# A block attention stage rebuilt around quarter-height matmuls, in an eight-layer kernel on one core

## The chip, the cores and the metric

The kernel runs on one core of one Trainium2 chip. The metric is the device time of one execution in microseconds (us), here the median of three. A core has five engines with queues of their own: TensorE (PE), VectorE (DVE), ScalarE (ACT), GpSimd (POOL) and SyncE (SP), which here only starts transfers.

## The reference

The program is a stack of eight layers over x, 16 batches of 128 tokens by 128 features, with a second input of the same shape as context. The layer that matters here is the second block attention (`L1_xattn`), third in the kernel's count (`layer2`). Its input is the normalised x for the queries and the context for keys and values. There are 16 heads of width 8. For each head and each of the two blocks of 64 keys a softmax of its own is taken, and the two results are added with the weights 1 and 2:

```
q = norm(x) @ Wq * 8**-0.5 ; k = ctx @ Wk ; v = ctx @ Wv         (16 heads of 8)
for each batch, head, block g of 64 keys:
    s = q @ k[g].T ;  p = exp(s - max(s)) ;  o_g = (p @ v[g]) / sum(p)
x += gate * ((o_0 + 2 * o_1) @ Wo)
```

The layer before it (`layer1`) is a small feed-forward layer (128 to 512 to 128), the one after it (`layer3`) a feed-forward layer with eight compared branches.

## The kernel before

Everything is written by hand: each engine has one list of instructions, and semaphores join them. Features lie on the 128 partitions and tokens in the free dimension, so xT is 128 by 2048, cut into four chunks of 512 (one PSUM bank of f32). PSUM has eight banks, `bank(0)` to `bank(7)`.

Each layer begins with `pe_norm`, `act_norm` and `dve_norm`: two matmuls per chunk (L192, L197), three ACT passes (L207, L211, L212) and one DVE product (L218).

`layer2` then projects keys and values (L538, L540) and splits k into a high and a low f16 part (L632 on ACT, L669 on DVE). To give each of the 16 heads its own rows, `spread_keys` writes, per batch and part, a 128 by 2048 f16 table of k times a head mask, on POOL (L623; on DVE for batch 0). POOL also carries one row gather (an indirect DMA, L808) ahead of each table: these 128 gathers in all fill `pe`, which `layer3` turns (L834) and `layer4` uses. POOL waits for the landing of one before it starts the next.

The attention runs in 32 half steps (`t`), each with 8 heads of one batch. A half step is: scores on PE (L571, 6 matmuls of 512 columns, tokens of the queries on partitions), maximum and subtraction on DVE (L682, L685), exp on ACT (L663), 8 transposes on PE (L581), two copies on ACT (L652), 8 matmuls of 18 columns on PE (L601) into `pv`. Per batch DVE then divides and adds (L695 to L699). Every four batches a query projection (L562), four transposes (L588) and the output projection (L593) come in between. `TURNS` is the order in which banks 4 and 5 are filled and copied.

Of the kernel before, what the change touches and what calls it, by code (L numbers as in the profile page):

```python
# [5 lines left out]
B, S, D = 16, 128, 128  # L6
# [27 lines left out]
def flamingo_kernel(nc, ins, out, stop=LAYERS):  # L34
# [5 lines left out]
    with ExitStack() as ctx:  # L40
# [16 lines left out]
        consts = sb("consts", [128, 5 * 128 + NH1 + 2 * NH2 + CAP + NH2 // 2])  # L57
# [3 lines left out]
        l1x_w = sb("l1x_w", [D, 4 * D])  # L61
# [37 lines left out]
        hm4 = consts[:, 640 + NH1 + 2 * NH2 + CAP:640 + NH1 + 2 * NH2 + CAP + NH2 // 2]  # L99
        l0f_w1 = work[:, 11264:11264 + F]  # L100
# [56 lines left out]
        A2 = sems("attn2", "vset k_ps v_ps k low v kblk s exp_in exp fill filled pv o")  # L157
# [16 lines left out]
        CEN = (4, 0, 0, 0, 4, 0, 3, 0)  # L174
        VAR = (2, 4, 6, 6, 0, 6, 0, 4)
# [266 lines left out]
        def pe_layer1(te):  # L442
            pe_norm(te, 1)
            loaded(te, "l0f")
            for c in range(NCH + 1):
                if c < NCH:
                    for f in range(FT):
                        if c:
                            te.wait_ge(F1["act"], FT * (c - 1) + f + 1)
                        te.matmul(bank(f), l0f_w1[:, f * 128:(f + 1) * 128], nT[:, cs(c)],  # L450
                                  start=True, stop=True).then_inc(F1["up"], 1)
                if c:
# [10 lines left out]
        def act_layer1(act, link):  # L463
# [7 lines left out]
            for c in range(NCH + 1):  # L471
                if c < NCH:
                    for f in range(FT):
                        act.wait_ge(F1["up"], FT * c + f + 1)
                        if c >= 2:
                            act.wait_ge(F1["down"], c - 1)
                        act.activation(hq[:, c % 2, f, :], bank(f), ACT.Relu, bias=col("l0f_b1", f),
                                       saturate=False).then_inc(F1["act"], 1)
                if c:
# [6 lines left out]
        def dve_layer1(dve, link):  # L486
            dve_norm(dve, 1)
            for c in range(NCH + 1):
                if c:
# [10 lines left out]
        WEIGHT1 = 2.0  # L500
        VW = 2 * (HD1 + 1)
        vext = wA[:, 0:B * NH1 * VW].rearrange("p (b h w) -> p b h w", b=B, h=NH1)
        kT = wA[:, B * NH1 * VW:B * NH1 * VW + T].bitcast(f16).rearrange("p (r n) -> p r n", r=2)
        qT = nT[:].bitcast(f16).rearrange("p (c r n) -> p c r n", c=NCH, r=2)
        kblk = work[:, 0:4096].bitcast(f16).rearrange("p (s r h k) -> p s r h k", s=2, r=2, h=NH1)
        Q_SCALE = HD1 ** -0.5
        pr = work[:, 4096:8192].rearrange("p (r h k) -> p r h k", r=2, h=NH1)
        prT = work[:, 8192:12288].rearrange("p (r h q) -> p r h q", r=2, h=NH1)
        mx = sm(0, NH1 * NBLK // 2)
        rs = sm(32, NH1 * NBLK)  # L510
        o_a = sm(64, 128).rearrange("p (h w) -> p h w", h=NH1)
        o_b = sm(192, 128).rearrange("p (h w) -> p h w", h=NH1)
        otok = sm(512, 512).rearrange("p (b d) -> p b d", b=BC)
        oT = sm(1024, 512)
        y2 = sm(1536, 512)

        HH = NH1 // 2
        STEPS = 2 * B
        CS = 2 * BC
        TURNS = []  # L520
        for _t in range(STEPS + 5):
            if _t == 0 or _t < STEPS - 1 and _t % CS == CS - 1:
                TURNS.append((_t, ("q", (_t + 1) // CS)))
            if 2 <= _t < STEPS + 2:
                TURNS += [(_t, ("t", _t - 2, j)) for j in range(2)]
            if _t >= CS + 3 and (_t - 3) % CS == 0:
                TURNS.append((_t, ("o", (_t - 3) // CS - 1)))
            if _t >= CS + 4 and (_t - 4) % CS == 0:
                TURNS.append((_t, ("y", (_t - 4) // CS - 1)))

        def fill_at(*what):
            return [w for _, w in TURNS].index(what) + 1

        def pe_layer2(te):
            pe_norm(te, 2)
            loaded(te, "l1x")
            for c in range(NCH):
                te.matmul(bank(c), l1x_w[:, D:2 * D], cT[:, cs(c)], start=True, stop=True).then_inc(A2["k_ps"], 1)  # L538
            for b in range(B):
                mm = te.matmul(bank(4 + b // BC)[:, (b % BC) * D:(b % BC + 1) * D], cT[:, tok(b)],  # L540
                               l1x_w[:, 2 * D:3 * D], start=True, stop=True)
                if b % BC == BC - 1:
                    mm.then_inc(A2["v_ps"], 1)
            te.wait_ge(A2["low"], NCH)
            te.wait_ge(A2["v"], 2 * NCH)

            def fill(*what):
                n = fill_at(*what) - 1
                if n >= 2:
                    te.wait_ge(A2["filled"], n - 1)  # L550
                    last = TURNS[n - 2][1]
                    if last[0] == "q":
                        te.wait_ge(A2["low"], NCH + last[1] + 1)
                return bank(4 + n % 2)


            for t in range(STEPS + 5):
                if t < STEPS:
                    b, j = t // 2, t % 2
                    if (t, ("q", (t + 1) // CS)) in TURNS:  # L560
                        c = (t + 1) // CS
                        te.matmul(fill("q", c), l1x_w[:, 0:D], nT[:, cs(c)], start=True, stop=True).then_inc(A2["fill"], 1)  # L562
                    if t % CS == 0:
                        te.wait_ge(A2["low"], NCH + t // CS + 1)
                    if b:
                        te.wait_ge(A2["kblk"], b)
                    if t >= 2:
                        te.wait_ge(A2["exp_in"], t - 1)
                    for n in range(2):
                        for i, (p, r) in enumerate(PARTS):  # L570
                            mm = te.matmul(bank(2 * j + n), qT[:, b // BC, p, b % BC * S:(b % BC + 1) * S],  # L571
                                           kblk[:, b % 2, r, HH * j + 4 * n:HH * j + 4 * n + 4, :], start=(i == 0), stop=(i == 2))
                    mm.then_inc(A2["s"], 1)
                if 2 <= t < STEPS + 2:
                    u = t - 2
                    a, j = u // 2, u % 2
                    te.wait_ge(A2["exp"], u + 1)
                    for n in range(2):
                        dst = fill("t", u, n)
                        for h in range(4):  # L580
                            mm = te.transpose(dst[:, h * S:(h + 1) * S], pr[:, a % 2, HH * j + 4 * n + h, :], ident)  # L581
                        mm.then_inc(A2["fill"], 1)
                if t >= CS + 3 and (t - 3) % CS == 0:
                    c = (t - 3) // CS - 1
                    te.wait_ge(A2["o"], BC * (c + 1))
                    dst = fill("o", c)
                    for n in range(BC):
                        mm = te.transpose(dst[:, n * S:(n + 1) * S], otok[:, n, :], ident)  # L588
                    mm.then_inc(A2["fill"], 1)
                if t >= CS + 4 and (t - 4) % CS == 0:  # L590
                    c = (t - 4) // CS - 1
                    te.wait_ge(A2["filled"], fill_at("o", c))
                    te.matmul(fill("y", c), l1x_w[:, 3 * D:4 * D], oT, start=True, stop=True).then_inc(A2["fill"], 1)  # L593
                if 3 <= t < STEPS + 3:
                    u = t - 3
                    a, j = u // 2, u % 2
                    te.wait_ge(A2["filled"], fill_at("t", u, 1))
                    if a >= 2 and j == 0:
                        te.wait_ge(A2["o"], a - 1)
                    for h in range(HH * j, HH * (j + 1)):  # L600
                        mm = te.matmul(bank(6 + a % 2)[:, h * VW:(h + 1) * VW], prT[:, a % 2, h, :], vext[:, a, h, :],  # L601
                                       start=True, stop=True)
                    if j:
                        mm.then_inc(A2["pv"], 1)

        def pool_layer2(pool, link):
            pool.wait_ge(s_x, NCH)
            link(pool.memset(wA[:, 0:B * NH1 * VW], 0.0))
            link(pool.memset(vext[0:64, :, :, HD1:HD1 + 1], 1.0))
            pool.memset(vext[64:128, :, :, VW - 1:VW], 1.0).then_inc(A2["vset"], 1)  # L610
            for b in range(1, B):
                pool.wait_ge(A2["low"], b // BC + 1)
                if b >= 2:
                    pool.wait_ge(A2["s"], 2 * (b - 1))
                spread_keys(pool, b).then_inc(A2["kblk"], 1)
            pool_gather(pool, IN_L0 + 2 * (B - 1), S)

        def spread_keys(eng, b):
            for r in range(2):
                if b:  # L620
# [1079 lines left out]
```

## Time and profile before

| | |
|---|---|
| time, median of 3 | 1003.61 us (1000.99 to 1004.13) |
| the profiled execution: its time, its span | 1002.72 us, 1000.7 us |
| PE, DVE, ACT, POOL busy | 87%, 66%, 58%, 35% of the span |
| mean granted TensorE clock | 0.921 of full speed |
| `layer1` from its first matmul | 235.7 us |
| `layer2`: norm begins, norm ends | 255.0 us, 264.6 us |
| first score, begin of the next layer | 277.1 us, 450.6 us |

The span is from the first to the last instruction; the execution's own time is 2.0 us longer. Starts are in microseconds from the start of the span. A f32 matmul stands in the trace as two records, a f16 matmul as one. PEld is the load of a matmul's fixed operand, which overlaps PE. The granted clock is 1.00 at 2.4 GHz and 0.50 at 1.2 GHz.

### The profile page before, as it was taken

The page shows a single profiled execution, that of the slowest core. Times are in us where ns is not written, and L with a number is a line of the kernel's source. Part 1 is how long each engine was busy: PE and PEld are TensorE (multiplying, and loading weights), DVE is VectorE, ACT ScalarE, POOL GpSimd, SP SyncE. Part 2 cuts the span into 40 slices and gives each one's busy share as a digit, 9 for nine tenths or more (in the row PEclk, how much of TensorE's full clock was granted, in tenths as well). Part 3 has the DMA queues.
Part 4 walks back from the last instruction along what each step waited for, and adds up shares of the span by engine and source line. Part 5 has one row for each costly group of instructions (what it writes and reads, how often), then busy time and mean ns, then how long its engine had stood idle before and what let it go on. Part 6 is the DMA issues. An engine that isn't in the chain of part 4 may idle for free.

```text
span 1000.7 us, 13965 instructions
## 1 busy us (share of the span) xinstructions
PE 872.9 (87%) x5417; PEld 574.6 (57%) x5417; DVE 663.9 (66%) x979; ACT 580.6 (58%) x994; POOL 354.2 (35%) x254
## 2 busy tenths in 40 slices
PE   4899999999779888999997699996889887989776
PEld 1576777763347667674555675553568764444322
DVE  3886767651557677654887667885677426776667
ACT  4797878756734444435447233453568565576464
POOL 1123233331589799833333022105693003000003
PEclk9899999998979799889998799887799998999888
DMA  6210000006000000000000000005000000000001
GB/s 215 63 61 20 20 22 23 23 22 95 9 14 14 11 14 14 14 22 24 21 25 1 1 1 1 1 1 213 0 1 1 2 1 0 1 0 1 1 0 42
DMA packets 12848, 25.35 MB, mean 25 GB/s; under 512 B 3560, under 2 KB 4848, under 8 KB 12528
## 3 DMA queue, kind: packets, MB, share of 16 engines
q1 hardware_dynamic: 8688, 16.07, 5.6%
q0 software_dynamic: 4096, 8.40, 3.3%
q8 instruction: 43, 0.70, 0.3%
q14 instruction: 21, 0.17, 0.1%
HBM read 23.41 MB, written 1.05 MB: 24 GB/s over the span
## 4 chain that ended last, share of the span: by engine, by line
PE 61%; DVE 22%; ACT 11%; issue 3%; POOL 1%; DMA 1%; SPq 0%; POOLq 0%; DVEq 0%; ACTq 0%
PE ps L317 8%; PE ps L289 8%; PE ps L728 6%; PE ps L601 4%; PE ps L571 4%; PE ps L867 3%; PE ps L192 2%; PE ps L581 2%; PE ps L1219 2%; DVE big L954 2%; PE ps L1189 2%; ACT nT L211 2%; ACT nT L212 2%; PE ps L450 2%; PE ps L197 1%
## 5 line engine op out<-in xcount | busy, mean ns | idle before, releaser
L808 POOL DMA_INDIRECT pe<-in_rpe,idx x128 | 132.6, 1036 | 274.2 <-DMA pe<-in_rpe,idx 197.2
L359 DVE TENSOR_TENSOR big<-l1f_w,big 128x512 f16<-128x512 f32 x128 | 87.3, 691 | 42.2 <-ACT big L346 39.7
L623 POOL TENSOR_TENSOR big<-big,consts 128x2048 f16<-128x2048 f16 x30 | 109.8, 3659 | 0.6
L345 ACT ACTIVATE l1f_w<-ps,wcols 128x512 f32<-128x512 f32 x128 | 90.1, 704 | 29.7 <-PE ps L289 27.2
L317 PEld LDWEIGHTS ps<-big 128*128 128x128 f16 x1536 | 89.8, 99 | 12.4 <-DVE big L359 5.3
L317 PE MATMUL ps<-big 128*128 128x128 f16 x1536 | 92.6, 221 | 4.7 <-DVE big L359 4.7
L289 PE MATMUL ps<-vx,big 128*128 128x512 f16 x384 | 91.6, 390 | 2.7 <-DVE nT L218 2.7
L346 ACT ACTIVATE big<-ps,wcols 128x512 f16<-128x512 f32 x128 | 90.6, 708 | 0.0
L601 PEld LDWEIGHTS ps<-big 128*128 128x128 f32 x512 | 66.1, 208 | 1.8 <-issue 1.0
L601 PE MATMUL ps<-big 128*128 128x18 f32 x512 | 65.1, 272 | 0.0
L289 PEld LDWEIGHTS ps<-vx,big 128*128 128x128 f16 x384 | 37.5, 101 | 44.0 <-issue 4.6
L652 ACT ACTIVATE big<-ps 128x512 f32<-128x512 f32 x64 | 35.5, 594 | 46.5 <-PE ps L581 46.5
L682 DVE TENSOR_REDUCE small<-ps 128x16 f32<-128x1024 f32 x32 | 39.0, 1220 | 31.4 <-PE ps L571 31.1
L728 PE MATMUL ps<-nT,l1f_w 128*128 128x512 f32 x128 | 57.7, 593 | 2.2 <-DVE nT L218 2.2
L1484 POOL TENSOR_TENSOR big<-l1f_w,big 128x512 f16<-128x512 f32 x8 | 10.6, 1331 | 138.4 <-ACT big L1521 138.4
L571 PE MATMUL ps<-big,nT 128*128 128x512 f16 x192 | 54.8, 430 | 5.0 <-POOL big L623 2.2
L663 ACT ACTIVATE big<-big 128x1024 f32<-128x1024 f32 x32 | 33.8, 1056 | 36.4 <-DVE big L685 36.4
L192 PE MATMUL ps<-xT,consts 128*128 128x512 f32 x64 | 40.2, 735 | 11.4 <-DMA xT<-in_xT 9.9
L936 ACT ACTIVATE big<-ps,small 128x128 f32<-128x128 f32 x128 | 34.9, 380 | 25.7 <-PE ps L894 25.7
L218 DVE TENSOR_TENSOR nT<-ps,nT 128x512 f32<-128x512 f32 x32 | 22.1, 691 | 40.8 <-ACT nT L212 40.7
L825 POOL TENSOR_TENSOR big<-nT,consts 128x512 f32<-128x512 f32 x16 | 16.8, 1059 | 83.2 <-PE ps L884 43.8
L581 PE MATMUL ps<-consts,big 128*128 128x128 f32 x256 | 38.5, 298 | 5.4 <-DVE nT L676 5.3
(307 smaller groups left out, 1869.4 us busy)
## 6 DMA issues: line engine op xcount, KB each, us to landing
big<-in_l0x_w SPq DMA_DIRECT2D x16, 256.0 KB, 3.3
pe<-in_l2f_w SPq DMA_DIRECT2D x16, 256.0 KB, 6.5
pe<-in_rpe,idx POOLq DMA_INDIRECT x128, 2.6
cT<-in_cT SPq DMA_DIRECT2D x1, 1024.0 KB, 9.7
l1f_w<-in_l1f_w SPq DMA_DIRECT2D x1, 1024.0 KB, 5.1
vx<-in_ctok SPq DMA_DIRECT2D x1, 1024.0 KB, 16.5
out_xT<-xT SPq DMA_DIRECT2D x4, 256.0 KB, 2.2
xT<-in_xT SPq DMA_DIRECT2D x1, 768.0 KB, 7.1
```

The costliest lines, as they stand in the source:

```text
L192: te.matmul(bank(CEN[i] + c), centre_w, xT[:, cs(c)], start=True, stop=True).then_inc(s_cen, 1)
L289: mm = te.matmul(bank(f), w16[:, e, a, f * 128:(f + 1) * 128], x16[:, c, b, :], start=(n == 0), stop=(n == 2))
L317: mm = te.matmul(bank(4 + k % 2)[:, t * D:(t + 1) * D], h16[:, k % 2, a, f, t * S:(t + 1) * S], w16[:, k % E, b, F + f * D:F + (f + 1) * D ...
L345: act.activation(h32[:, f, :], bank(f), ACT.Relu, bias=b, scale=1 / W_UP)
L346: act.activation(h16[:, k % 2, 0, f, :], bank(f), ACT.Relu, bias=b, scale=1 / W_UP).then_inc(M0["act"], 1)
L359: dve.tensor_tensor(h16[:, k % 2, 1, f, :], h32[:, f, :], h16[:, k % 2, 0, f, :], SUB).then_inc(M0["lo"], 1)
L571: mm = te.matmul(bank(2 * j + n), qT[:, b // BC, p, b % BC * S:(b % BC + 1) * S], kblk[:, b % 2, r, HH * j + 4 * n:HH * j + 4 * n + 4, :], ...
L581: mm = te.transpose(dst[:, h * S:(h + 1) * S], pr[:, a % 2, HH * j + 4 * n + h, :], ident)
L601: mm = te.matmul(bank(6 + a % 2)[:, h * VW:(h + 1) * VW], prT[:, a % 2, h, :], vext[:, a, h, :], start=True, stop=True)
L623: ins_ = eng.tensor_tensor(kblk[:, b % 2, r, :, :], kT[:, r, tok(b)].unsqueeze(1).to_broadcast([128, NH1, S]), hm16.unsqueeze(2).to_broadc ...
L728: mm = te.matmul(bank(at + r), l1f_w[:, w * D:(w + 1) * D], nT[:, cs(2 * (k // NC) + r)], start=True, stop=True)
L808: pool.indirect_dma_start(out=pe[:, v * D:(v + 1) * D], out_offset=None, in_=ins["rpe"], in_offset=bass.IndirectOffsetOnAxis(ap=idx[:, v:v ...
```

## The change

1. **Keys and values** are projected in `layer1`, after each chunk's four first matmuls (`pe_keys`, `dve_keys`). v is written once per key block, zero outside of it (16 columns a head instead of 18, without columns of ones).
2. **Scores in row groups.** The 16 heads are cut into four quarters `t` of four heads, which lie on 32 partitions each (`quad(t)`). k and q are spread with a mask over four heads (tables of 128 by 1024, both parts in one instruction, both on POOL). A score matmul has K = 32 rows, 512 columns, and bank `t`.
3. **Second scores.** The first scores are only used for the maxima (`dve_reduce`). PE turns the 8 maxima of each quarter into rows (`pe_maxima`), DVE spreads them with a minus sign (`dve_maxima`, mblk), and the scores are computed again with keys on partitions (`pe_turned`), with a fourth, f32 matmul that adds minus the maximum. ACT takes exp straight from PSUM (banks 4 and 5). Subtraction, transposes and copies are gone.
4. **Values in column groups.** 16 matmuls (M = 16, 128 columns, f32) and 4 for the sums (M = 32, 512 columns, f32) write the partitions 32t to 32t + 31 of banks 6 and 7. DVE takes the reciprocal of all 128 by 512 sums and multiplies.
5. **Projection.** The output stands transposed already; it is projected by 4 f32 matmuls of 512 columns per four batches, against weights with each row of Wo laid out twice, and added to x from PSUM.
6. Banks of the norm of `layer3` are changed; three constant tables and the three further weight blocks are loaded with the others (170 and 384 columns more).

```diff
-        CEN = (4, 0, 0, 0, 4, 0, 3, 0)
-        VAR = (2, 4, 6, 6, 0, 6, 0, 4)
+        CEN = (4, 0, 0, 4, 4, 0, 3, 0)
+        VAR = (2, 4, 6, 2, 0, 6, 0, 4)
...
+        def pe_keys(te, c):
...
+            te.matmul(bank(6), l1x_w[:, D:2 * D], cT[:, cs(c)], start=True, stop=True).then_inc(A2["proj_ps"], 1)
+            for t in range(BC):
+                mm = te.matmul(bank(7)[:, t * D:(t + 1) * D], cT[:, tok(c * BC + t)], l1x_w[:, 2 * D:3 * D], start=True, stop=True)
+            mm.then_inc(A2["proj_ps"], 1)
...
+        def pe_scores(te, b, t, part):
+            p, r = PARTS[part]
+            return te.matmul(bank(t), qT[quad(t), b // BC, p, b % BC * S:(b % BC + 1) * S], kblk[quad(t), b % KS, r, :, :],
+                             start=(part == 0), stop=(part == 2))
+
+        def pe_turned(te, b, t, part):
+            if part == 3:
+                return te.matmul(bank(4 + t % 2), to_keys[quad(t), :], mblk[quad(t), b % 2, :, :], start=False, stop=True)
+            p, r = PARTS[part]
+            return te.matmul(bank(4 + t % 2), kT[quad(t), p, tok(b)], qblk1[quad(t), b % QS, r, :, :],
+                             start=(part == 0), stop=False)
+
+        def pe_maxima(te, b):
+            te.wait_ge(A2["mx"], 2 * b + 2)
+            te.transpose(bank(2)[:, 0:128], mxp[:, b % 2, :, :].rearrange("p t w -> p (t w)"), ident).then_inc(A2["mT"], 1)
+
+        def pe_values(te, b):
+            te.wait_ge(A2["exp"], 2 * b + 2)
+            if b:
+                te.wait_ge(A2["on"], b)
+            for j in range(4):
+                for t in range(4):
+                    te.matmul(bank(6)[32 * t:32 * t + 2 * HD1, j * S:(j + 1) * S], vext[:, b, 4 * t + j, :], pr[:, b % 2, t, j, :],
+                              start=True, stop=True)
+            for t in range(4):
+                mm = te.matmul(bank(7)[quad(t), :], sum_w, pr[:, b % 2, t, :, :], start=True, stop=True)
+            mm.then_inc(A2["pv"], 1)
...
+            for b in range(B + 2):
+                if b + 2 < B and (b + 2) % BC == 0:
+                    te.wait_ge(A2["mx"], 2 * b + 3)
+                    pe_queries(te, (b + 2) // BC)
+                if b >= BC + 1 and (b - BC - 1) % BC == 0:
+                    if b + 1 < B:
+                        te.wait_ge(A2["mx"], 2 * b + 3)
+                    pe_project(te, (b - BC - 1) // BC)
+                if b < B:
+                    te.wait_ge(A2["mblk"], b + 1)
+                    te.wait_ge(A2["qblk"], b + 1)
+                    if b:
+                        te.wait_ge(A2["exp"], 2 * b)
+                    for part in range(4):
+                        for t in (0, 1):
+                            mm = pe_turned(te, b, t, part)
+                        if part == 3:
+                            mm.then_inc(A2["st"], 1)
+                        elif b + 1 < B:
+                            for t in (2, 3):
+                                mm = pe_scores(te, b + 1, t, part)
+                            if part == 2:
+                                mm.then_inc(A2["s"], 1)
+                if 1 <= b <= B:
+                    pe_values(te, b - 1)
+                if b + 1 < B:
+                    pe_maxima(te, b + 1)
+                if b < B:
+                    te.wait_ge(A2["exp"], 2 * b + 1)
...
+                    for part in range(4):
+                        for t in (2, 3):
+                            mm = pe_turned(te, b, t, part)
...
+                            for t in (0, 1):
+                                mm = pe_scores(te, b + 2, t, part)
...
+                for u in range(2):
+                    act.wait_ge(A2["st"], 2 * b + u + 1)
+                    act.activation(pr[:, b % 2, 2 * u:2 * u + 2, :, :].rearrange("p t j q -> p (t j q)"), ps[:, 2048:3072],
+                                   ACT.Exp).then_inc(A2["exp"], 1)
...
+            for b in range(B + 2):
+                if b + 2 < B and (b + 2) % BC == 0:
+                    dve_queries(dve, (b + 2) // BC)
+                if b >= BC + 1 and (b - BC - 1) % BC == 0:
+                    c = (b - BC - 1) // BC
+                    dve.wait_ge(A2["y_ps"], c + 1)
+                    dve.scalar_tensor_tensor(xT[:, cs(c)], bank(0), gt[:, 2:3], xT[:, cs(c)], MUL, ADD).then_inc(s_x, 1)
+                if b + 1 < B:
+                    dve_reduce(dve, b + 1, 1)
+                    dve_maxima(dve, b + 1)
+                if 1 <= b <= B:
+                    a = b - 1
                     dve.wait_ge(A2["pv"], a + 1)
...
+                    link(dve.reciprocal(rsum, bank(7)))
+                    dve.tensor_tensor(on[:, a // BC % 2, :, a % BC, :], bank(6).rearrange("p (j q) -> p j q", j=4),
+                                      rsum.rearrange("p (j q) -> p j q", j=4), MUL).then_inc(A2["on"], 1)
+                if b + 2 < B:
+                    dve_reduce(dve, b + 2, 0)
```

PE's order at the heart of `layer2` before, two and a half half steps (L571 the scores, L581 the transposes of the exponentials, L601 the values):

```order
L571 MATMUL ps<-big,nT 128x512 x6
L581 MATMUL ps<-consts,big 128x128 x8
L601 MATMUL ps<-big 128x18 x8
L571 MATMUL ps<-big,nT 128x512 x6
L581 MATMUL ps<-consts,big 128x128 x8
```

And PE's order in the same place now, from the end of the first bundle of batch 1 to the queries ahead of batch 2 (L557 the f32 matmul of the maxima, L572 and L575 values and sums of batch 0, L564 the transpose of the maxima of batch 2, L559 the turned scores of batch 1, L552 the first scores of batch 3, L548 a query projection):

```order
L557 MATMUL ps<-big,consts 128x512 x2
L572 MATMUL ps<-big 16x128 x16
L575 MATMUL ps<-big,consts 32x512 x4
L564 MATMUL ps<-consts,small 128x128
L559 MATMUL ps<-big 128x512 x2
L552 MATMUL ps<-big,nT 128x512 x2
L559 MATMUL ps<-big 128x512 x2
L552 MATMUL ps<-big,nT 128x512 x2
L559 MATMUL ps<-big 128x512 x2
L552 MATMUL ps<-big,nT 128x512 x2
L557 MATMUL ps<-big,consts 128x512 x2
L548 MATMUL ps<-nT,l1x_w 128x512
```

Before, the three kinds of work of a half step follow each other. Now turned scores and first scores alternate two by two in a bundle that ends with the two f32 matmuls of the maxima, values and sums stand between the two bundles of a batch, and a projection stands ahead of the first.

DVE's order now in the same place (L703 half of the maxima, L709 mblk, L735 and L736 the division, L699 the low part of a chunk of queries):

```order
L703 TENSOR_REDUCE small<-ps 128x2x8
L699 SCALAR_TENSOR_TENSOR nT<-ps,nT 128x512
L703 TENSOR_REDUCE small<-ps 128x2x8
L709 TENSOR_TENSOR big<-ps,consts 128x512
L735 RECIPROCAL small<-ps 128x512
L736 TENSOR_TENSOR big<-ps,small 128x4x128
L703 TENSOR_REDUCE small<-ps 128x2x8 x2
```

The division, a reciprocal of 32 columns before, is now one of 512, and it stands ahead of the reduction of the next scores.

## Rows read from the trace of the kernel before

**Rows 1.** The page, busy time of each engine and what shares the chain that ended last.

```profile
PE 872.9 (87%) x5417; PEld 574.6 (57%) x5417; DVE 663.9 (66%) x979; ACT 580.6 (58%) x994; POOL 354.2 (35%) x254
...
PE 61%; DVE 22%; ACT 11%; issue 3%; POOL 1%; DMA 1%; SPq 0%; POOLq 0%; DVEq 0%; ACTq 0%
```

**Rows 2.** The chain that ended last, `layer2` to the next layer: start, length, what.

```profile
264.58 3.71 PE ps L538 x8
...
269.64 6.80 DVE big L623 x2
...
277.10 4.23 PE ps L571 x12
...
305.46 1.30 PE ps L571 x6
...
450.63 3.41 PE ps L192 x4
```

**Rows 3.** Timeline of PE in `layer2`: start, length, instruction, idle before it.

```profile
317.18 1.86 PE L601 MATMUL ps<-big 128*128 128x18 f32 x16
...
321.05 1.86 PE L601 MATMUL ps<-big 128*128 128x18 f32 x16
...
331.53 1.12 PE L588 MATMUL ps<-consts,small 128*128 128x128 f32 x4 [2.57 <-DVE small L699]
332.44 3.44 PE L601 MATMUL ps<-big 128*128 128x18 f32 x16
```

**Rows 4.** Windows of 2 us: length, PE busy (instructions), granted clock, DMA share, GB/s.

```profile
332.00:334.00 2.00, 2.00 (x12) 0.50 0.13 33
...
338.00:340.00 2.00, 2.00 (x10) 0.50 0.09 23
...
354.00:356.00 2.00, 0.00 (x0) 1.00 0.00 0
...
360.00:362.00 2.00, 2.00 (x9) 0.51 0.04 10
```

**Rows 5.** Timeline of POOL at the end of `layer2` and in `layer3`.

```profile
417.20 0.99 POOL L808 DMA_INDIRECT pe<-in_rpe,idx  x1 [0.16 <-issue]
418.21 3.61 POOL L623 TENSOR_TENSOR big<-big,consts 128x2048 f16<-128x2048 f16 x1
...
426.76 0.98 POOL L808 DMA_INDIRECT pe<-in_rpe,idx  x1 [0.16 <-issue]
...
522.65 0.94 POOL L808 DMA_INDIRECT pe<-in_rpe,idx  x1 [1.90 <-DMA pe<-in_rpe,idx]
```

**Rows 6.** Groups by line on PE: shapes, records | busy us, mean ns | idle.

```profile
L317 PE MATMUL ps<-big 128*128 128x128 f16 x1536 | 92.6, 221 | 4.7 <-DVE big L359 4.7
...
L540 PE MATMUL ps<-l1x_w,cT 128*128 128x128 f32 x32 | 3.7, 275 | 0.0
L538 PE MATMUL ps<-cT,l1x_w 128*128 128x512 f32 x8 | 3.7, 605 | 2.2 <-DVE nT L218 2.2
```

**Rows 7.** Window of `layer1`: PE, PEld, DVE, ACT, POOL busy, clock, DMA share, GB/s.

```profile
235.70:255.00 19.30, 19.26 (x49) 8.52 (x50) 1.76 (x3) 13.16 (x20) 4.87 (x6) 0.91 0.31 35
```

**Rows 8.** Groups by line on DVE.

```profile
L682 DVE TENSOR_REDUCE small<-ps 128x16 f32<-128x1024 f32 x32 | 39.0, 1220 | 31.4 <-PE ps L571 31.1
...
L695 DVE RECIPROCAL small<-ps 128x32 f32<-128x32 f32 x16 | 5.7, 358 | 16.6 <-PE ps L601 16.1
...
L669 DVE TENSOR_TENSOR big<-ps,big 128x512 f16<-128x512 f32 x4 | 2.8, 692 | 2.3 <-ACT big L632 2.2
...
L1445 DVE RECIPROCAL small<-small 128x4 f32<-128x4 f32 x12 | 2.1, 178 | 0.4
```

**Rows 9.** The exponential, ACT in `layer2`.

```profile
L663 ACT ACTIVATE big<-big 128x1024 f32<-128x1024 f32 x32 | 33.8, 1056 | 36.4 <-DVE big L685 36.4
```

**Rows 10.** The chain that ended last, the last matmuls of `layer3` before the sixteenth turn (L834).

```profile
526.86 3.45 PE ps L728 x8
```

More of the change, by code:

```diff
@@ L156, in flamingo_kernel @@
         F1 = sems("ffn1", "w2q up act down o16")
-        A2 = sems("attn2", "vset k_ps v_ps k low v kblk s exp_in exp fill filled pv o")
+        A2 = sems("attn2", "proj_ps hi low v kblk qblk s mx mT mblk st exp pv on y_ps")
         F3 = sems("ffn3", "sel comp take best cand picked")
@@ L512, in flamingo_kernel @@
[L512 to L529, printed above, removed]
@@ L531, in fill_at @@
-        def fill_at(*what):
-            return [w for _, w in TURNS].index(what) + 1
+        KS, QS = 3, 2
+        qblk1 = work[:, 0:1024].bitcast(f16).rearrange("p (s r j q) -> p s r j q", s=QS, r=2, j=4)
+        mblk = work[:, 1024:2048].rearrange("p (s j q) -> p s j q", s=2, j=4)
+        kblk = work[:, 2560:4096].bitcast(f16).rearrange("p (s r j k) -> p s r j k", s=KS, r=2, j=4)
+        pr = work[:, 4096:8192].rearrange("p (s t j q) -> p s t j q", s=2, t=4, j=4)
+        on = work[:, 8192:12288].rearrange("p (s j b q) -> p s j b q", s=2, j=4, b=BC)
@@ new lines, in pe_queries @@
+        def pe_queries(te, c):
+            te.matmul(bank(1), l1x_w[:, 0:D], nT[:, cs(c)], start=True, stop=True).then_inc(A2["proj_ps"], 1)
+        def pe_scores(te, b, t, part):
[8 more added lines that the diff above has]
+                             start=(part == 0), stop=False)
@@ L534, in pe_layer2, with pe_project @@
+        def pe_project(te, c):
+            te.wait_ge(A2["on"], BC * (c + 1))
+            for j in range(4):
+                mm = te.matmul(bank(0), l1x_w[:, (3 + j) * D:(4 + j) * D], on[:, c % 2, j, :, :], start=(j == 0), stop=(j == 3))
+            mm.then_inc(A2["y_ps"], 1)
         def pe_layer2(te):
+            te.wait_ge(A2["low"], NCH)
+            te.wait_ge(A2["v"], NCH)
             pe_norm(te, 2)
-            loaded(te, "l1x")
-            for c in range(NCH):
-                te.matmul(bank(c), l1x_w[:, D:2 * D], cT[:, cs(c)], start=True, stop=True).then_inc(A2["k_ps"], 1)
@@ L539, in pe_layer2 @@
-            for b in range(B):
[L540 to L554, printed above, removed]
@@ L557, in pe_layer2 @@
[L557 to L604, printed above, removed]
@@ L618, in spread_keys @@
[L618 to L625 removed]
+            pe_queries(te, 0)
+            te.wait_ge(A2["low"], NCH + 1)
@@ new lines, in pe_layer2 @@
+            te.wait_ge(A2["v"], NCH)
+            te.wait_ge(A2["kblk"], 1)
+            for u in range(2):
+                for part in range(3):
+                    for t in (2 * u, 2 * u + 1):
+                        mm = pe_scores(te, 0, t, part)
+                mm.then_inc(A2["s"], 1)
+            te.wait_ge(A2["kblk"], 2)
+            te.wait_ge(A2["mx"], 1)
+            for part in range(3):
+                for t in (0, 1):
+                    mm = pe_scores(te, 1, t, part)
+            mm.then_inc(A2["s"], 1)
@@ new lines, in pool_layer2 @@
+        def pool_layer2(pool, link):
+            for b in range(KS - 1):
+                pool_keys(pool, b)
+            for b in range(B):
+                if b:
+                    v = IN_L0 + 2 * (b - 1)
+                    pool_gather(pool, v, v + 1)
+                if b + KS - 1 < B:
+                    pool_keys(pool, b + KS - 1)
+                if b:
+                    pool_gather(pool, v + 1, v + 2)
+                pool.wait_ge(A2["low"], NCH + b // BC + 1)
+                if b >= QS:
+                    pool.wait_ge(A2["st"], 2 * (b - QS) + 2)
+                pool_spread(pool, qblk1[:, b % QS, :, :, :],
+                            qT[:, b // BC, :, b % BC * S:(b % BC + 1) * S]).then_inc(A2["qblk"], 1)
+            pool_gather(pool, IN_L0 + 2 * (B - 1), S)
@@ L665, in dve_layer2, with dve_maxima @@
+        def dve_maxima(dve, b):
+            dve.wait_ge(A2["mT"], b + 1)
+            dve.tensor_tensor(mblk[:, b % 2, :, :], bank(2)[:, 0:128].unsqueeze(1).to_broadcast([128, 4, S]),
+                              minus4.unsqueeze(2).to_broadcast([128, 4, S]), MUL).then_inc(A2["mblk"], 1)
         def dve_layer2(dve, link):
             dve_norm(dve, 2)
-            for c in range(NCH):
-                dve.wait_ge(A2["k"], c + 1)
-                dve.tensor_tensor(kT[:, 1, cs(c)], bank(c), kT[:, 0, cs(c)], SUB).then_inc(A2["low"], 1)
```

191 lines of the change are left out of this document (94 added, 97 removed).

## The prediction

> **What bounds the kernel now.** I read first the page's chain: PE holds 61% of it and is busy for 87% of the span [rows 1], so the reader is to look at what PE does, and at what it waits for where it does not. The chain in order of time gives the piece that the change rebuilds: the norm of `layer2` ends at 264.58, the next layer begins at 450.63, which is 186.1 us [rows 2]. Within it the first score starts at 277.10: 3.71 us of key projections, then 6.80 us in which DVE spreads the keys of batch 0 [rows 2]. From there 173.5 us go to 16 batches, 10.8 us for each.
>
> Three things share these 10.8 us. PE alone needs less: undisturbed half steps start 3.87 us apart (317.18 and 321.05), 7.75 us a batch [rows 3]. POOL needs 9.56 us: from the gather at 417.20 to the one at 426.76 lie two gathers of 0.99 and two tables of 3.61 us with hardly a pause [rows 5]. And PE pays for pauses twice. It waited 2.57 us at 331.53, and 16 records of L601 then took 3.44 us where they take 1.86 [rows 3]; the clock stayed at half from 332 to 340 [rows 4]. It idled from 354 to 356 and ran at half at 360 [rows 4]. So the stage is held by POOL and by restarts, with PE close behind.
>
> **Part 1, the start.** Keys and values move into `layer1`: 8 records of L538 in 3.7 us, 32 of L540 in 3.7 us [rows 6]. PE is busy there for 19.26 of 19.30 us [rows 7], so all 7.4 us are paid. ACT's four copies and DVE's eight new passes are covered: ACT has 6 us free and DVE 17 [rows 7]. In exchange `layer2` starts sooner. From the end of the norm: a query projection 0.86 (two records of 0.43, from L538's 3.44 for 8 in steady flow, here 3.7 with the first one's start, [rows 6]), a copy and the low part 0.6 + 0.7, two bundles of first scores with three reductions of 1.22 behind them, mblk 0.69 [rows 8], and about 0.9 us of handing over: the loop begins 7.8 us behind the norm. POOL's first tables are made before that, beside the norm.
>
> **Part 2, what a batch costs on PE.** I count slots. A f16 matmul of 512 columns takes 0.216 (six in 1.30, [rows 2]), a f32 one of 512 columns 0.86 and one of 128 columns 0.233 (both L538 and L540, [rows 6]); the last two stand in the trace as two records each, one behind the other. One after another the new batch would need 24 x 0.216 for scores, 4 x 0.86 for the maxima, 16 x 0.233 for values, 4 x 0.86 for sums, 0.1 for the transpose: 15.9 us. That is twice today's 7.75. The whole change rests on matmuls in different quarters of the array running at once, and no row here shows that. The bounds: each waits for the one before (0.216 us apart), or only issue counts, of which L317 gives 0.060 us (1536 records in 92.6 us, [rows 6]). I take the low end for f16, since nothing that two such matmuls share (queue, weight load) takes longer than those 0.060: a round of four costs one slot, 0.22 to 0.24.
>
> For f32 I take less, and this is the choice that decides. PE starts its matmuls in the order of the program. The second record of quarter 0 has to wait for the first one on the same rows, and the first record of quarter 1 stands behind it. So the chain is 0a, 0b with 1a, 1b with 2a, and so on: n matmuls take n + 1 half slots, where free overlap would take a quarter of 2n.
>
> - A bundle of turned and first scores: three f16 rounds, 0.66, and two f32 matmuls in three half slots of 0.43, 1.29: together **1.95**. Two bundles a batch.
> - Values: 17 half slots of 0.117, 1.99; sums: five of 0.43, 2.15: **4.1**.
> - Transpose of the maxima and two changes of shape: **0.25**.
> - ACT's exp of the second bundle reads banks 4 and 5, which the next batch's first bundle overwrites. Nothing stands between: 1.06 [rows 9] and 0.25 to hand over, **1.3** of idle PE. The exp of the first bundle hides behind the values.
>
> Sum 2 x 1.95 + 4.1 + 0.25 + 1.3 = **9.6 us** a batch.
>
> The Trainium skill, "TensorE: Matmul & The Clock Gate", "Part 3: Packing small matmuls — row/col tiling", says that matmuls on different groups of rows do overlap, four of them with 512 columns being 3.07 times as fast, and that matmuls start in program order. No run here shows the factor yet; by it a round of four would cost 0.28 instead of 0.22 and a batch 0.4 us more.
>
> **Part 3, DVE.** This engine gets a long instruction. A reciprocal of 4 columns takes 178 ns, of 32 columns 358 [rows 8]: 6.4 ns for each further column (6.25 by the one between). For 512 that gives 178 + 508 x 6.3 = **3.4 us**, worked out far beyond the rows, but they lie on a line. With two reductions of 1.22, mblk 0.69 and the product 0.69 [rows 8] DVE has 7.2 us a batch. In most batches this hides beside PE. Six batches are different: ahead of a query projection (b = 2, 6, 10) and of an output projection (b = 5, 9, 13) PE waits for the reduction that stands behind the division in DVE's list. Counted from the end of the sums: transpose 0.25, mblk 0.7, reciprocal 3.4, product 0.7, reduction 1.22 and some handing over, 6.4 us; PE is there after 0.25 + 1.95 + 1.3 = 3.5. Each costs **2.9 us** more, and PE then has stood still for 4.2.
>
> The Trainium skill, "VectorE: DVE Perf Modes", section "Walkthrough: the 8-slice pipeline in each mode", has the reciprocal divide with a repeat count of 8. If that meant eight times the 1.03 ns of a plain column (L682 against L669, [rows 8]), it would be 4.2 us and each of the six waits 0.8 us longer; the rows give 6.3 ns a column and I go by them.
>
> **Part 4, POOL and the gathers.** A table of 1024 costs half of 3.61, 1.8; two with two gathers 5.6, and gathers alone allow 2.82 apart (34 of them from 426.76 to 522.65, [rows 5]). POOL falls well under 9.6 and leaves the path. What is late next would be `layer3`, whose sixteenth turn needs the last gather: it starts at 522.65, and the turn comes at 530.3 [rows 5, 10], some 5 us after the landing. The last 34 gathers stay tied to the end of POOL's tables, which now wait for batch 13 as they did before; with two batches and a tail of 12 us behind that, the slack remains. I take nothing for it. If `layer2` were to end over 5 us sooner behind the last table, that cover would be gone.
>
> **Part 5, the sum.** The loop: 16 x 9.6 = 154, less 4.1 (batch 0 has no values before it), plus 6 x 2.9 = 17, plus three output projections of 3.44 and three query projections of 0.86, 13: **180**. The end: values 4.1, division and handing over 4.3, last projection 3.4: **12**. `layer2` from the norm's end: 7.8 + 180 + 12 = 200 against 186.1: +14. `layer1` +7.4. The clock: PE stands 4.2 us six times; after 2.6 us it lost 8 us of full clock, after 2.2 some 3 [rows 4], of which half is time lost where PE is the bound. I take 1.5 to 4 us each, 2.5 in the middle, 15, and 3.4 for the last projection at half clock, which follows such a pause: +18. The larger constants are in the first load; I take nothing. Together +40 us on the profiled execution's 1002.7, which is 0.9 below the median: **1042 us**. With 1.5 and 4 it is 1036 to 1051; with 20% on the slots either way 1022 to 1063.
>
> **Rivals.**
>
> - **f32 overlaps freely.** Bundle 0.66 + 0.86 = 1.5, values and sums 1.8. PE would need 5.1 + 1.3, and DVE's ring becomes the bound: reduction 1.22, transpose and handing over 0.35, mblk 0.7, division 4.15, reduction 1.22: 7.6. The loop is 16 x 7.6 - 4 + 3 x 2.3 + 3 x 4.2 = 137, the end 9.5, in all 154: 32 us under today's 186. With `layer1`'s 7.4 that leaves 24 us gain, 979, and 996 where the clock takes 17 back. For it: nothing in rows forbids it. Against: the two records. It decides where a batch falls under about 9 us. Chance 0.25.
> - **In between, on the fast side.** The pairs of records as I say, but the clock holds, POOL's and DVE's collisions of today count for more than I gave them, or the sums overlap with the values: 985 to 1001. Chance 0.10.
> - **No overlap at all.** 15.9 + 1.3 + 0.2 a batch: 7.8 us more than my 9.6, sixteen times, some +120 on mine: about 1150. Chance 0.07.
> - **It cancels.** The loop comes out at 155 to 160 and pays exactly for `layer1`: within 3 us (0.3%, what a measurement here can tell from no change). Chance 0.06.
>
> My forecast has the rest, 0.52, and its own range is 1020 to 1065. The range that should hold 8 in 10 runs from 984 to 1070; what lies outside is part of the free overlap and the serial case. Faster 0.34, same 0.06, slower 0.60.
>
> **What the next profile would show.** Right: four scores (L552, L559) that start within some 30 ns of each other; second records of L557, L572 and L575 that start with the next quarter's first; L735 at 3.4 us; PE waiting 1.3 us for ACT once a batch and about 4 for DVE L703 ahead of L548 and L581; the half clock behind those; `layer1` 7.4 us longer; POOL no longer named in PE's waits. Wrong: sums of 4 x 512 columns in under 1.1 us, or values in 1 us (the first rival); records of L552 0.2 us apart (no overlap); a DVE that is never waited for.

## The result and the profile after

The changed kernel takes 1025.47 us, median of four runs (1021.42 to 1031.97), against 1002.3 us before: ratio 1.024, interval 1.018 to 1.030. It is slower by some 23 us, where 40 were forecast. The profiled execution has a span of 1029.7 us, the longest of the four, so its own distances are used below, not its end. Even these vary: over the same matmuls of `layer2` the profiles of two kernels differ by 8 us (207.9 and 199.6 in the table below), so what a change is worth is taken from the medians.

The page, as in [rows 1]: busy times, and the chain's shares.

```profile
PE 870.6 (85%) x5633; PEld 517.6 (50%) x5633; DVE 663.6 (64%) x935; ACT 534.9 (52%) x914; POOL 297.1 (29%) x253
...
PE 59%; DVE 25%; ACT 11%; issue 2%; DMA 1%; SPq 0%; POOL 0%; POOLq 0%; DVEq 0%; ACTq 0%
```

PE is as busy as before, and POOL lost 57 us. The chain in order of time, as in [rows 2] (start, length, what):

```profile
237.88 5.11 PE ps L456 x8
...
257.59 6.13 DVE xT L503
...
275.41 2.09 PE ps L548 x2
...
312.96 3.28 DVE small L735
...
320.32 3.28 DVE small L735
...
327.69 3.28 DVE small L735
...
342.72 3.28 DVE small L735
...
473.67 1.72 PE ps L198 x4
```

The norm of `layer2` ends at 275.41 (its first query projection, L548), the next layer begins at 473.67: 198.3 us where it was 186.1 [rows 2]. `layer1` with the norm behind it takes 37.5 us (237.88 to 275.41) instead of 28.8 (235.74 to 264.58). The rest of the 29 us between the two spans lies outside, 2.1 ahead and 6 behind. `layer3` takes as long as before (82 us to the norm of `layer4`), so the 6 lie in the layers behind it, which the change does not touch, and what made the 2.1 was not looked for. The median moved by 23.

DVE's reciprocal L735 is the clock of the chain: 7.37 us apart in undisturbed batches, 15.0 us apart (327.69 to 342.72) where a projection comes in. One such place on the timeline (start, length, instruction, idle before it):

```profile
327.61 3.35 DVE L735 RECIPROCAL small<-ps 128x512 f32<-128x512 f32 x1
...
331.60 1.22 DVE L703 TENSOR_REDUCE small<-ps 128x16 f32<-128x1024 f32 x1
...
332.87 5.40 PE L581 MATMUL ps<-big,l1x_w 128*128 128x512 f32 x8 [4.30 <-DVE small L703]
...
338.20 0.39 PE L559 MATMUL ps<-big 32*128 32x512 f16 x2
...
338.20 0.39 PE L552 MATMUL ps<-big,nT 32*128 32x512 f16 x2
...
338.43 0.38 PE L559 MATMUL ps<-big 32*128 32x512 f16 x2
...
338.86 1.02 PE L557 MATMUL ps<-big,consts 32*128 32x512 f32 x4
...
339.81 1.07 PE L572 MATMUL ps<-big 128*16 128x128 f32 x32
...
340.69 1.04 PE L575 MATMUL ps<-big,consts 128*32 128x512 f32 x8
...
341.66 0.33 PE L564 MATMUL ps<-consts,small 128*128 128x128 f32 x1
```

Three things are to be read here. PE stands 4.30 us for the reduction L703, which stands behind the reciprocal in DVE's list. The projection after it takes 5.40 us instead of 3.44, so the clock had fallen. And the small matmuls are fast: a round of four f16 (two L559, two L552) every 0.21 to 0.23 us, two f32 of 512 columns in 0.86, 16 values in 1.0, four sums in 0.9. A bundle is 1.61 us long (338.20 to 339.81), values and sums together 1.85 (to 341.66). Each group takes about the time that one quarter's share of it would take alone: it overlaps freely.

Windows of the changed kernel (length; PE, PEld, DVE, ACT, POOL busy; granted clock; DMA), the whole stage, two undisturbed batches, and a batch behind a pause:

```profile
275.40:473.70 198.30, 147.20 (x1209) 58.90 (x1210) 117.44 (x89) 35.13 (x36) 96.07 (x71) 0.75 0.06 15
...
312.88:327.61 14.73, 11.08 (x152) 4.89 (x148) 13.82 (x12) 4.09 (x4) 11.57 (x8) 1.00 0.08 19
...
342.64:357.63 14.99, 10.69 (x81) 3.82 (x77) 7.70 (x8) 2.64 (x3) 5.78 (x4) 0.66 0.05 14
```

And the same stage of the kernel before:

```profile
264.60:450.60 186.00, 164.45 (x1033) 126.05 (x1034) 129.51 (x141) 82.34 (x119) 150.25 (x69) 0.87 0.06 14
```

The mean clock of the stage fell from 0.87 to 0.75. In the two batches from 312.88 DVE is busy for 13.82 of 14.73 us, PE for 11.08: at full clock DVE bounds them.

### The profile page after: what moved, and what is told of

It reads as the page before. It is cut to its first block, busy times and chain, and to the rows that moved or that the text cites. A ratio compares the mean times of both kernels' runs of the same rounds, so it can differ in the third digit from the quotient of the medians.

```text
span 1029.7 us, 14149 instructions
## 1 busy us (share of the span) xinstructions
PE 870.6 (85%) x5633; PEld 517.6 (50%) x5633; DVE 663.6 (64%) x935; ACT 534.9 (52%) x914; POOL 297.1 (29%) x253
## 4 chain that ended last, share of the span: by engine, by line
PE 59%; DVE 25%; ACT 11%; issue 2%; DMA 1%; SPq 0%; POOL 0%; POOLq 0%; DVEq 0%; ACTq 0%
PE ps L323 8%; PE ps L295 8%; PE ps L764 6%; DVE small L735 4%; PE ps L903 3%; PE ps L581 2%; PE ps L557 2%; PE ps L1255 2%; PE ps L198 2%; PE ps L572 2%; DVE small L703 2%; PE ps L559 2%; DVE big L990 2%; PE ps L1225 2%; ACT nT L217 2%
## 5 line engine op out<-in xcount | busy, mean ns | idle before, releaser
L844 POOL DMA_INDIRECT pe<-in_rpe,idx x128 | 129.6, 1013 | 261.1 <-DMA pe<-in_rpe,idx 207.7
L694 ACT ACTIVATE big<-ps 128x1024 f32<-128x1024 f32 x32 | 32.7, 1023 | 129.5 <-PE ps L557 129.5
L295 PE MATMUL ps<-vx,big 128*128 128x512 f16 x384 | 94.1, 397 | 2.7 <-DVE nT L224 2.7
L764 PE MATMUL ps<-nT,l1f_w 128*128 128x512 f32 x128 | 59.3, 607 | 2.2 <-DVE nT L224 2.2
L735 DVE RECIPROCAL small<-ps 128x512 f32<-128x512 f32 x16 | 53.6, 3349 | 8.3 <-PE ps L575 8.3
L653 POOL TENSOR_TENSOR big<-nT,consts 128x1024 f16<-128x1024 f16 x16 | 30.4, 1900 | 55.7 <-PE ps L557 39.9
L703 DVE TENSOR_REDUCE small<-ps 128x16 f32<-128x1024 f32 x32 | 38.3, 1218 | 8.6 <-PE ps L552 8.3
L559 PE MATMUL ps<-big 32*128 32x512 f16 x192 | 32.0, 444 | 13.2 <-ACT big L694 11.7
L203 PE MATMUL ps<-nT,consts 128*128 128x512 f32 x64 | 37.1, 665 | 4.1 <-ACT nT L213 4.1
L213 ACT ACTIVATE nT<-ps 128x512 f32<-128x512 f32 x32 | 18.7, 587 | 41.8 <-PE ps L198 41.7
L557 PE MATMUL ps<-big,consts 32*128 32x512 f32 x128 | 40.0, 704 | 0.0
```

The lines of the kernel that those rows point to most:

```text
L295: mm = te.matmul(bank(f), w16[:, e, a, f * 128:(f + 1) * 128], x16[:, c, b, :], start=(n == 0), stop=(n == 2))
L557: return te.matmul(bank(4 + t % 2), to_keys[quad(t), :], mblk[quad(t), b % 2, :, :], start=False, stop=True)
L559: return te.matmul(bank(4 + t % 2), kT[quad(t), p, tok(b)], qblk1[quad(t), b % QS, r, :, :], start=(part == 0), stop=False)
L703: dve.tensor_reduce(mxp[:, b % 2, 2 * u:2 * u + 2, 0:8], ps[:, 1024 * u:1024 * (u + 1)].rearrange("p (t g k) -> p t g k", t=2, k=BLK), AX, ...
L735: link(dve.reciprocal(rsum, bank(7)))
L764: mm = te.matmul(bank(at + r), l1f_w[:, w * D:(w + 1) * D], nT[:, cs(2 * (k // NC) + r)], start=True, stop=True)
```

## The experiments

Theory 1: pauses of PE drop its clock, and this costs more than the pauses. Theory 2: the reciprocal on DVE makes the six long waits and sets the 7.4 us. Theory 3: POOL's first tables hold up the end of `layer1`. The rival from the prediction's sum, that f32 matmuls cost half slots in program order, is measured by the fifth. "Stage" in the table is the distance in each profile from the end of `layer2`'s norm to the first matmul behind `layer3`'s norm (L764), so it is some 10 us longer than the 198.3 and 186.1 above. It is one execution each.

| kernel | median us | ratio to before (interval) | stage us |
|---|---|---|---|
| before | 1002.3 | 1 | 197.4 |
| changed | 1025.5 | 1.024 (1.018 to 1.030) | 207.9 |
| spare matmuls in the pauses | 1000.7 | 0.997 (0.993 to 1.001) | 183.0 |
| reduction ahead of division | 1007.2 | 1.002 (0.997 to 1.006) | 187.8 |
| reciprocal on ACT | 974.1 | 0.972 (0.966 to 0.978) | 159.2 |
| POOL's tables later | 1022.6 | 1.020 (1.015 to 1.026) | 199.6 |
| quarter by quarter | 1051.9 | 1.053 (1.047 to 1.059) | 230.4 |
| ACT and later tables | 968.4 | 0.971 (0.966 to 0.976) | 155.8 |
| the same with spare matmuls | 974.7 | 0.975 (0.970 to 0.980) | 158.9 |

The kernel before was run with each set; its medians there were 1003.6 (first four) and 998.9 (last three), so the ratios compare better than the medians.

**Spare matmuls in the pauses.**

```diff
+        def keep_busy(te, b):
+            te.wait_ge(A2["mblk"], b + 1)
+            for n in range(18):
+                te.matmul(bank(3), kT[:, 0, 0:128], kT[:, 0, 0:CW], start=True, stop=True)
...
+                    keep_busy(te, b)
                     te.wait_ge(A2["mx"], 2 * b + 3)
                     pe_queries(te, (b + 2) // BC)
```

> The changed kernel with 18 spare f16 matmuls of 512 columns (3.9 us at full clock), whose result is overwritten, in each of the six places where PE waits for DVE's reduction ahead of a projection. They start when mblk of the batch is there and fit into the 4.3 us of idle PE. Theory 1 (the clock: each such pause drops TensorE to half speed, and the work behind it pays 3 to 5 us): no half clock behind the six places, the output projections at 3.44 instead of 5.4 us and more, 18 to 28 us faster than the changed kernel, ratio to before 0.995 to 1.007. Rival (the clock falls for another reason, such as the 1.3 us pauses for ACT or the quarter-height matmuls themselves): clock still near 0.75 in the stage, time within 5 us of the changed kernel or slower.

The kernel got 25 us faster by 108 matmuls that compute nothing. Its window of the stage, as above, to the end of the last projection:

```profile
274.40:447.90 173.50, 144.81 (x1317) 60.16 (x1318) 117.18 (x90) 35.17 (x36) 94.34 (x69) 0.89 0.06 16
```

173.5 us instead of 198.3 at a clock of 0.89 instead of 0.75, with DVE's work unchanged (117.2 us). Theory 1 holds: six filled pauses give back as much as the change had lost. More than half of the half clock that is left lies at the start of the stage, where nothing was filled (window of 22 us, granted clock 0.50):

```profile
276.40:298.40 22.00, 16.61 (x108) 5.59 (x108) 9.03 (x9) 3.07 (x3) 17.38 (x12) 0.50 0.07 19
```

The kernel stood 0.3% under the kernel before, which the interval does not tell from no change.

**Reduction ahead of division.**

```diff
+        AHEAD = (2, 5, 6, 9, 10, 13)
...
                     dve.wait_ge(A2["pv"], a + 1)
+                    if b + 1 in AHEAD:
+                        dve_reduce(dve, b + 2, 0)
                     link(dve.reciprocal(rsum, bank(7)))
...
-                if b + 2 < B:
+                if b + 2 < B and b + 1 not in AHEAD:
                     dve_reduce(dve, b + 2, 0)
```

> Only DVE's order is changed: ahead of the six projections the reduction of the next scores stands before the division, not behind it. Theory 1 and 2 together (the wait of 4.3 us comes from the division ahead in DVE's list, and drops the clock): the waits for L703 go from 4.3 us to under 1.5, each place saves 3 us and another 2 to 4 of half clock, 25 to 40 us faster than the changed kernel, ratio to before 0.985 to 1.0. Rival (the wait only moves: the values of the next batch then wait for the product behind the division): new waits of L572 for L736 of 3 us and less than 8 us gained.

18 us under the changed kernel, between the 25 to 40 of the theory and the 8 of the rival. What PE waited for (waiter, what for: us in total, times, longest), first in the changed kernel:

```profile
PE ps L581 <- DVE small L703: 12.9, 3, 4.3
PE ps L548 <- DVE small L703: 12.9, 3, 4.3
PE ps L559 <- ACT big L694: 11.7, 10, 1.2
```

and then in this one (L740 is the product behind the reciprocal):

```profile
PE ps L581 <- DVE big L740: 18.2, 4, 4.7
PE ps L559 <- ACT big L694: 11.7, 10, 1.2
PE ps L572 <- DVE big L740: 9.1, 11, 2.5
PE ps L548 <- DVE small L703: 1.6, 3, 0.6
```

The query projections wait 1.6 instead of 12.9 us. The output projections need the product itself, and wait as long as before behind the same reciprocal. Part of the rival holds too: the values (L572) now wait 9.1 us for the product, 4.1 in the changed kernel, up to 2.5 at a time. Moving it helps where its result isn't needed at once, and nowhere else.

**The reciprocal on ACT.**

```diff
+        def act_divide(act, link, a):
+            act.wait_ge(A2["pv"], a + 1)
+            link(act.activation(rsum, bank(7), ACT.Ln))
+            act.activation(rsum, rsum, ACT.Exp, scale=-1.0).then_inc(A2["rcp"], 1)
...
                 for u in range(2):
+                    if u and b:
+                        act_divide(act, link, b - 1)
                     act.wait_ge(A2["st"], 2 * b + u + 1)
...
-                    link(dve.reciprocal(rsum, bank(7)))
+                    dve.wait_ge(A2["rcp"], a + 1)
```

> The reciprocal of the 512 sums moves from DVE to ACT, as Ln and Exp with scale -1 (about 0.7 and 0.63 us), between the two exponentials of a batch. Theory 2 (DVE's 3.35 us reciprocal sets the 7.4 us period and the six waits): the period between projections falls from 7.4 to PE's own ring of 6.3 to 6.6 us, the six waits to under 1.5 us, in all 35 to 50 us faster than the changed kernel, ratio to before 0.975 to 0.99. Rival (PE with its f32 matmuls in pairs of half slots is the bound, 8.3 us a batch and more): under 10 us gained and PE without pauses.

51 us under the changed kernel, just past the 50 expected, and 2.8% under the one before. The chain in an undisturbed batch of this kernel (L701 the exponential):

```profile
305.73 0.88 PE ps L557 x4
...
306.63 1.03 ACT big L701
...
308.62 0.85 PE ps L557 x4
309.48 1.00 PE ps L572 x32
310.48 0.86 PE ps L575 x8
...
312.35 0.88 PE ps L557 x4
```

The batch takes 6.62 us (305.73 to 312.35), no DVE in it: 5.4 us of PE and 1.2 of waiting for ACT's exponential. Theory 2 holds, and the rival with half slots (8.3 us of PE a batch at least) is ruled out. PE's waits for the reduction at the six places are 1.4 us at most instead of 4.3, so this run takes away the pauses as well as the 7.4 us period; the 51 us are both together.

**POOL's tables later.**

```diff
         def pool_layer2(pool, link):
+            pool.wait_ge(s_x, 2 * NCH)
```

> POOL makes its first tables only when layer 1 has ended. Theory 3 (the update of x at the end of layer 1 waits for POOL's tables of 1.9 us, L503 takes 2.5 us instead of 0.75 in three of four cases): L503 back at 0.75 us, layer 1 some 3 to 5 us shorter, nothing lost behind since POOL has the 9.6 us of the norm, ratio to before 1.018 to 1.021. Rival (L503 is long for another reason or hides): same time as the changed kernel, 1.024.

The changed kernel's update of x (minimum, median, maximum in ns), then this one's:

```profile
L503 DVE SCALAR_TENSOR_TENSOR xT<-big,gt,xT x4: 736/745/6134, 251.5 to 266.0; 128x512 f32<-128x512 f16 x4
```

```profile
L503 DVE SCALAR_TENSOR_TENSOR xT<-big,gt,xT x4: 750/752/752, 250.8 to 263.7; 128x512 f32<-128x512 f16 x4
```

One of four updates took 6.13 us beside POOL's tables and takes 0.75 without them, so the mechanism is there; the expectation's 2.5 us in three of four cases was a mean of one long update and short ones. From the first matmul of `layer1` to the norm's end it gives 35.9 us instead of 37.5. But the long update does not always reach the end of the layer: the kernels with spare matmuls and quarter by quarter keep the early tables, have an update of 3.2 and of 6.5 us, and take 35.9 and 35.7 us there as well. The ratio moved by less than the intervals: it is not shown that the time of the kernel changed, here or with the reciprocal on ACT.

**Quarter by quarter.**

```diff
-            for j in range(4):
-                for t in range(4):
+            for t in range(4):
+                for j in range(4):
                     te.matmul(bank(6)[32 * t:32 * t + 2 * HD1, j * S:(j + 1) * S], vext[:, b, 4 * t + j, :], pr[:, b % 2, t, j, :],
...
+                    if b + 1 < B:
+                        for t in (2, 3):
+                            for part in range(3):
+                                mm = pe_scores(te, b + 1, t, part)
+                        mm.then_inc(A2["s"], 1)
+                    for t in (0, 1):
+                        for part in range(4):
+                            mm = pe_turned(te, b, t, part)
+                    mm.then_inc(A2["st"], 1)
```

> The same matmuls as in the changed kernel, but in PE's program quarter by quarter: in a bundle first the three parts of one quarter's first scores, then of the other, then the four parts of each quarter's turned scores, and the 16 value matmuls four by four of one quarter. Neighbours then share their rows or columns and only the seams can overlap. What the trace of the changed kernel shows (a round of four f16 in 0.21 us, two f32 in 0.86, 16 values in 1.00, four sums in 0.86: free overlap between quarters) says that this order costs a bundle 12 x 0.215 + 4 x 0.43 = 4.3 instead of 1.6 us and the values 3.7 instead of 1.0: 8 us a batch on PE, of which DVE's 7.4 us ring hides about 1: 95 to 120 us slower than the changed kernel, ratio to before 1.11 to 1.15. If overlap did little here, as with in-order half slots for f32, bundles would already cost much of that and the loss be 40 to 70 us.

26 us over the changed kernel, where either reading expected 40 or more. Its order in the program is six L552, then three L559 and one L557, twice. Its timeline (start, length, instruction):

```profile
344.89 0.40 PE L552 MATMUL ps<-big,nT 32*128 32x512 f16 x2
344.91 0.38 PE L559 MATMUL ps<-big 32*128 32x512 f16 x1
345.12 0.39 PE L552 MATMUL ps<-big,nT 32*128 32x512 f16 x2
345.14 0.39 PE L559 MATMUL ps<-big 32*128 32x512 f16 x2
345.33 0.39 PE L552 MATMUL ps<-big,nT 32*128 32x512 f16 x2
345.35 0.39 PE L559 MATMUL ps<-big 32*128 32x512 f16 x2
345.57 0.59 PE L557 MATMUL ps<-big,consts 32*128 32x512 f32 x1
...
346.75 2.08 PE L572 MATMUL ps<-big 128*16 128x128 f32 x29
348.56 0.63 PE L575 MATMUL ps<-big,consts 128*32 128x512 f32 x3
348.67 0.49 PE L572 MATMUL ps<-big 128*16 128x128 f32 x3
```

The first turned score L559 starts 0.02 us after the first L552, though six L552 stand before it in the program. In these rows a matmul starts beside those of the other quarters, even when they stand ahead of it. So the order of the program, on which both expectations rest, hardly matters to scores: a bundle takes 1.86 us (344.89 to 346.75) instead of 1.61 (338.20 to 339.81), where one quarter after another would give 4.3. The 16 values, two records each with short columns, take 2.0 us instead of 1.0: they overlap in part only. Why these and not the scores was not tested. Whether TensorE's queue does this or a later step of the build, these runs do not tell.

**Both together, and with spare matmuls.** `act_divide` and the later tables; then also `keep_busy` with 12 matmuls.

> The reciprocal on ACT and POOL's first tables after layer 1, together. Theories 2 and 3 add up: 2 to 4 us under the kernel with the reciprocal on ACT alone, ratio to before 0.968 to 0.971. Rival (the late tables then hold up the first scores): no gain or a loss of some us.

> As the one before, and 12 spare f16 matmuls of 512 columns (2.6 us) in the six places. With the reciprocal on ACT PE still idles about 2.8 us there and the output projection after it takes 5.4 instead of 3.44 us. Theory 1 (the clock): projections back at 3.44 us, 6 to 12 us less than without the spare matmuls, ratio to before 0.957 to 0.964. Rival: the pauses are short enough by now, the spare matmuls overshoot them and cost up to 3 us.

The first is the fastest median, 968.4 us, 2.9% under the kernel before; its gain over the reciprocal on ACT alone is not told apart. With the spare matmuls the output projections are back at full clock (592 ns each; the longest took 1061 without them):

```profile
L581 PE MATMUL ps<-big,l1x_w x32: 592/592/697, 325.2 to 422.6; 128*128 128x512 f32 x32
```

But the stage is no shorter (158.9 against 155.8), and the ratio is 0.975 against 0.971, with intervals that overlap. The 6 to 12 us expected of the clock did not come. That fits the rival: without the spare matmuls PE waited at most 1.4 us for L712 in those places, so 2.6 us of them overshoot that wait and seem to take what they win.

The first of the two also meets a new limit, in `layer3`. The shares of its chain, and the last two turns (L879), which need the gathers:

```profile
PE 54%; DVE 20%; ACT 12%; DMA 10%; issue 4%; POOL 0%; SPq 0%; POOLq 0%; DVEq 0%; ACTq 0%
```

```profile
485.74 1.04 PE L879 MATMUL ps<-consts,pe 128*128 128x128 f32 x8
490.91 1.09 PE L879 MATMUL ps<-consts,pe 128*128 128x128 f32 x8 [0.69 <-DMA pe<-in_rpe,idx]
```

The last turn comes 5.17 us behind the one before, 4.31 in the other kernels, because it waits for the last gather. That costs under 1 us here. But a stage made still shorter behind POOL's last table could not pass its gain on, unless the gathers came sooner too: the cover that the prediction put at some 5 us is used up.

## Why the prediction was right, and where its sum was off

**The sign and the waits were right, the sign in part by luck.** PE waits 4.3 us at six places for the reduction behind the division (4.2 forecast), the reciprocal takes 3.35 us (3.4), the exp pause is 1.2 (1.3), POOL leaves the path, and `layer3`'s last gather has more slack than before: it starts at 536.9, and the turn comes at 553.0. But the main term of the sum, the 9.6 us of a batch, was 2.2 us too long, and the clock was put too small; the two errors partly cancel. With the right batch and the prediction's own clock the sum is that of its first rival, 996 us and faster than before. It is the clock that makes the kernel slower.

The sum for the profiled execution was 1042 us, the execution took 1031.97. In it the stage was put at 200 us and 18 for the clock, and took 198.3, 20 less. `layer1` cost 1.3 more than forecast, and the 8 us ahead of it and behind the stage were in no term.

**The f32 half slots were wrong.** The step that failed is "the first record of quarter 1 stands behind it". Measured: bundle 1.61 instead of 1.95, values and sums 1.85 instead of 4.1. PE needs 5.4 us a batch, not 8.3. Here the first rival was close in every term of a batch (bundle 1.5, values and sums 1.8): it gave 7.6 us with DVE's ring as the bound, and it is 7.37. The Trainium skill ("TensorE: Matmul & The Clock Gate", "Part 3: Packing small matmuls — row/col tiling") is right on the overlap; its factor of 3.07 for four is about 4 here, a round every 0.21 us. What the same section says of the order, that matmuls start as the program has them, the quarter-by-quarter run does not bear out (a start 0.02 us behind the first of six that stand ahead of it; the queue or a step of the build), and the half slots were built on it.

**The clock was taken too small, and this made up for it.** The sum had 15 us for six pauses and 3.4 for the end. The spare matmuls, which fill only the six, win 25 us. The stage also begins at half speed, here and in the profiles of all seven variants. Windows of 2 us from the norm's end on (length, PE busy, clock, DMA) show 0.50 in all of the first eleven, of which two stand for them:

```profile
276.00:278.00 2.00, 1.49 (x2) 0.50 0.00 0
...
296.00:298.00 2.00, 2.00 (x28) 0.50 0.14 33
```

With free overlap and full clock the first rival had 154 us for the stage from the norm's end to the next layer, and 171 with the clock; it took 198.3. Of these 44 us more, that experiment shows 25 to be the clock behind the six pauses. The other 19 were not taken apart; the start at half speed has a part in them.

**`layer1`** costs 8.7 us in the profile, 7.4 forecast. What was not among the terms is the update beside POOL's tables: in this profile PE stands 1.8 us ahead of the norm's first matmuls behind it. In two of the other kernels with early tables this cost nothing.

**The reciprocal** decides the outcome. The prediction priced it right and saw its six waits; that it would bound every other batch too stood only with the rival. Moved to ACT, which is busy for 35 of the stage's 198 us, the same rebuild is 2.8% faster than the kernel before.

## What to carry to other kernels

When matmuls are packed into quarters, ask at once which engine is next: here four in the time of one moved the bound to a 128 by 512 reciprocal on VectorE, at 6.2 ns a column, while ScalarE was busy for 35 of 198 us. Price a pause of TensorE of some 4 us by what runs at half clock behind it; here it cost about as much again (25 us over six pauses). When a sum comes out near the measured time, compare its terms too: here two errors hid each other. A spare matmul in a pause is a cheap test of how much of a loss is the clock, but take the pause away where you can.

## What the hardware did unexpectedly

- Matmuls on different quarters of the array started out of the order of the program: 0.02 us apart with five others between them in the list. Whether the queue or the build does it is open.
- Four f16 matmuls of 32 rows and 512 columns ran in 0.21 us, and f32 ones, two records each, overlapped as freely: four sums in 0.86 us on four column groups.
- A DVE instruction that reads two tiles of SBUF (L503) took 6.13 instead of 0.75 us while POOL made three tables of 1.9 us (257.55 to 263.17). L709, with one operand in PSUM, kept its 0.69 us within such a table:

```profile
288.14 1.91 POOL L653 TENSOR_TENSOR big<-big,consts 128x1024 f16<-128x1024 f16 x1
...
288.77 0.69 DVE L709 TENSOR_TENSOR big<-ps,consts 128x512 f32<-128x512 f32 x1 [0.87 <-PE ps L564]
```
